# A recurrent stage with its state summed and transposed in two halves, and the shuffle moved

## The chip, the cores and the metric

The kernel runs on one core of a Trainium2 chip. The metric is the device time of one execution in microseconds; before the change it is 3043.02 us, the median of three runs (3042.71 to 3047.3). The engines that matter here are TensorE (PE, matrix products), VectorE (DVE, elementwise work, 32x32 transposes, shuffles between partitions), ScalarE (ACT, sigmoid and tanh), GpSimd (POOL, elementwise work) and SyncE (SP, transfers).

## The reference

The input x has the shape (16, 256, 512), the condition (16, 512). Four blocks are added to x one after the other: an attention over 8 heads, a causal depthwise convolution with 16 taps, a GRU, and an attention over 16 heads. The change touches the GRU alone. It runs over the 256 positions of the second axis, with 16 rows (the batch) and a state h of 512 columns that starts as the condition:

```python
def cell(h, x):
    gi = x @ W_ih + b_ih          # (16, 512) @ (512, 1536)
    gh = h @ W_hh + b_hh
    i_r, i_z, i_n = jnp.split(gi, 3, axis=-1)
    h_r, h_z, h_n = jnp.split(gh, 3, axis=-1)
    r = jax.nn.sigmoid(i_r + h_r)
    z = jax.nn.sigmoid(i_z + h_z)
    n = jnp.tanh(i_n + r * h_n)
    h_new = (1.0 - z) * n + z * h
    return (h_new, h_new)
x = x + _L2_cond_ref(cond_2048, x, L2_cond_W_ih, L2_cond_W_hh, ...)
```

All of it is computed in float32.

## The kernel before

The kernel has four parts in a row: a short set-up, the first attention (`l0_part`), the recurrent stage (`gru_part`), the second attention (`l3_part`). Each part writes out the work of every engine by hand, in order, and binds them with semaphores; there is no planner. A `wait` puts a condition ahead of the next instruction of its engine. The first wait is carried by the instruction itself; further waits are instructions of the engine's sequencer (`EVENT_SEMAPHORE`). Inside hardware loops the values waited for are computed in registers from the loop's variable.

In `gru_part` the 512 columns of a gate are laid out as four groups j of 32 partitions by 128 columns: column 128c + 32j + f of a gate lies at partitions 32j to 32j+31 and free column 32c + f (`group_of`). Each group holds 32 rows: the batch at two time steps (a pair). So each gate is one tile of 128 x 128 in PSUM, filled by four products per k (one for each j), each with a stationary operand of 16 or 32 columns and a moving weight of 128 columns. The even step of a pair (p = 0) uses rows 0 to 15, the odd one (p = 1) rows 16 to 31.

A step t does the following.

- TensorE (`recur`, line 829 on) waits until the turned state `hT` of step t is there (`hT_ready`), and adds h @ W_hh to the gates: 16 products for r, 16 for the hidden part of n, 16 for z, in this order, each over k = 0 to 3 and j = 0 to 3. A product in float32 is two records in the profile, so a gate is 32 records. Then `feed` (line 807 on) adds bias and x @ W_ih for the next pair, six parts a step, from the staged tile `x_st`; its first part of a pair waits for GpSimd's staging.
- ScalarE (line 856 on) takes the sigmoid of r (864), the tanh of a (868) and the sigmoid of z (871).
- VectorE (`step`, line 899 on) computes m = r * (hidden part of n) (907), a = input part of n + m, written to PSUM (911), d = h_swap - n (914), e = d * z (917), h = n + e (919), and turns h in 32x32 blocks into `hT` (922). `hT` has four blocks of columns, one for each k of the next step's products. The transpose waits for `added`, GpSimd's count of read states, and for `h_done`. Then it shuffles h into `h_swap`, with the two halves of 16 rows in each group exchanged (924), so that the next step's rows meet their own state. After that come convolution taps for a later chunk of 32 steps (`conv_tap`, 891): 64 taps are shared over 30 of the 32 steps, so most steps have two, four have three, and the last two of a chunk have none. The last pair of a chunk takes the maxima of the next chunk instead (`greatest`, 897). The last chunk has no taps. VectorE's and GpSimd's loops run over the six middle chunks; the first and last chunks are written out. TensorE's and ScalarE's loops have four steps.
- GpSimd adds the state to x (`add`, 770), once `hT_ready` tells that the transpose of the step is done, and stages the inputs of the next pair (`stage`, 756), once a pair.

Of the kernel before, what the change touches and what calls it, by code (L numbers as in the profile page):

```python
# [25 lines left out]
ALU = mybir.AluOpType  # L26
AX_X = mybir.AxisListType.X

P = 128
B, C, T = 16, 256, 512  # L30
CC, TC = C // P, T // P
# [6 lines left out]
QW = 32  # L38
# [7 lines left out]
def wait(eng, sem, value):  # L46

    if not (isinstance(value, int) and value <= 0):
        eng.wait_ge(sem, value)
# [642 lines left out]
def gru_part(nc, g):  # L692
# [6 lines left out]
    HALF = B  # L699
    SWAP = [(i + HALF) % QW for i in range(QW)]  # L700
    with ExitStack() as ctx:
# [41 lines left out]
        @block.gpsimd  # L743
        def _(pool):
            pool.memset(bias[:, :, :], 0.0).then_inc(setup, 1)
            pool.memset(h_swap[:, :], 0.0).then_inc(setup, 1)
            pool.memset(hT[:, :, :, :], 0.0).then_inc(setup, 1)
            pool.wait_ge(setup, 3)

            pool.tensor_copy(hT[:, 0, :, HALF:QW], g.condT[:, :, :]).then_inc(hT0_ready, 1)  # L750

            def stage(pair, par):


                wait(pool, x_used, pair - 1)
                pool.tensor_copy(x_st[:, par, :, :, :], g.xT[:, :, :, bass.ds(2 * pair, 2)].rearrange("p k b t -> p k t b"))\
                    .then_inc(x_ready, 1)

            def add(t, p):

                q = 1 - p
                if isinstance(t, int):
                    wait(pool, hT_ready, t + 1)
                else:

                    count = pool.snap(pool.to_reg(t + 1))
                    wait(pool, hT_ready, count)
                    t = pool.snap(pool.to_reg(count - 1))
                dst = g.xT[:, :, :, bass.ds(t, 1)].rearrange("p k b o -> p k (b o)")
                pool.tensor_tensor(dst, dst, hT[:, q, :, HALF:QW], ALU.add).then_inc(added, 1)  # L770

            def pair_steps(pair, par, more=True, greatest=0):
                if more:
                    stage(pair + 1, 1 - par)
                wait(pool, max_done, greatest)
                for p in range(2):
                    add(2 * pair + p, p)

            def chunk(n, last=False):
                for q in range(PAIRS):  # L780
                    if q == PAIRS - 1 and not last:
                        pool.wait_ge(conv_done, CONV * (n + 1))
                    pair_steps(PAIRS * n + q, q % 2, not (last and q == PAIRS - 1), TC * (n + 1) if q == 0 else 0)

            pool.wait_ge(copied, 1)
            stage(0, 0)
            chunk(0)
            with pool.Fori(1, CHUNKS - 1) as n:
                chunk(n)
            chunk(CHUNKS - 1, last=True)  # L790
# [11 lines left out]
        @block.tensor  # L802
        def _(pe):
            pe.wait_ge(g.gru_w_loaded, 16 * 2 * TC * GATES)
            pe.wait_ge(bias_loaded, 16 * 2 * GATES)
            pe.wait_ge(hT0_ready, 1)
            pe.wait_ge(ones_ready, 1)

            def feed(pair, par, gate, ks):

                out, done, slots = ((r_ps[par], r_done, slice(0, 1)), (n_ps[par], a_done, slice(1, 3)),
                                    (z_ps[par], z_done, slice(3, 4)))[gate]
                if 0 in ks:
                    if gate == 0:
                        wait(pe, x_ready, pair + 1)

                    wait(pe, done, 2 * (pair - 1))
                    for j in range(TC):
                        pe.matmul(out[QW * j:QW * j + QW, 0:(slots.stop - slots.start) * P], ones[:, :],
                                  bias[:, slots, :].rearrange("p g (c j f) -> p j g c f", c=TC, j=TC)[:, j],  # L820
                                  start=True, stop=True, skip_group_check=True)
                for k in ks:
                    for j in range(TC):
                        last = pe.matmul(out[QW * j:QW * j + QW, 0:P], x_st[:, par, k, :, :],  # L824
                                         group_of(wi[:, k, gate, :], j), start=False, stop=True, skip_group_check=True)
                if gate == 2 and TC - 1 in ks:
                    last.then_inc(x_used, 1)

            def recur(t, p, par):


                wait(pe, hT_ready, t)
                rows = HALF if p == 0 else QW
                state = slice(QW - rows, QW)
                for out, cols, gate, done in ((r_ps[par], slice(0, P), 0, r_in), (n_ps[par], slice(P, 2 * P), 1, n_in),
                                              (z_ps[par], slice(0, P), 2, z_in)):
                    for k in range(TC):
                        for j in range(TC):
                            last = pe.matmul(out[QW * j:QW * j + rows, cols], hT[:, p, k, state],  # L839
                                             group_of(wh[:, k, gate, :], j), start=False, stop=True, skip_group_check=True)  # L840
                    last.then_inc(done, 1)

            def step(pair, par, more):

                for p in range(2):
                    t = 2 * pair + p
                    recur(t, p, par)
                    parts = [(pair + 1, 1 - par, (6 * p + i) // 4, ((6 * p + i) % 4,)) for i in range(6)] if more else []
                    for part in parts:
                        feed(*part)  # L850

            for gate in range(GATES):
                feed(0, 0, gate, range(TC))
            loop(pe, step)

        @block.scalar
        def _(act):
            def step(pair, par, more):
                for p in range(2):
                    t = 2 * pair + p  # L860
                    wait(act, r_in, t + 1)

                    wait(act, m_done, t)
                    act.activation(r_sb[:, :], r_ps[par][:, 0:P], ACT.Sigmoid).then_inc(r_done, 1)  # L864
                    wait(act, a_done, t + 1)

                    wait(act, h_done, t)
                    act.activation(n_sb[:, :], a_ps[:, 0:P], ACT.Tanh).then_inc(n_done, 1)  # L868
                    wait(act, z_in, t + 1)
                    wait(act, e_done, t)  # L870
                    act.activation(z_sb[:, :], z_ps[par][:, 0:P], ACT.Sigmoid).then_inc(z_done, 1)

            loop(act, step)

        @block.vector
        def _(dve):
# [24 lines left out]
            def step(pair, par, taps, after=()):  # L901
                gates = n_ps[par]
                for p in range(2):
                    t = 2 * pair + p
                    wait(dve, n_in, t + 1)
                    wait(dve, r_done, t + 1)
                    dve.tensor_tensor(m_sb[:, :], gates[:, P:2 * P], r_sb[:, :], ALU.mult).then_inc(m_done, 1)  # L907
                    wait(dve, m_done, t + 1)

                    wait(dve, n_done, t)  # L910
                    dve.tensor_tensor(a_ps[:, 0:P], gates[:, 0:P], m_sb[:, :], ALU.add).then_inc(a_done, 1)  # L911
                    wait(dve, n_done, t + 1)
                    wait(dve, swap_done, t)
                    dve.tensor_tensor(d_sb[:, :], h_swap[:, :], n_sb[:, :], ALU.subtract).then_inc(d_done, 1)
                    wait(dve, d_done, t + 1)
                    wait(dve, z_done, t + 1)
                    dve.tensor_tensor(e_sb[:, :], d_sb[:, :], z_sb[:, :], ALU.mult).then_inc(e_done, 1)
                    wait(dve, e_done, t + 1)
                    dve.tensor_tensor(h_sb[:, :], n_sb[:, :], e_sb[:, :], ALU.add).then_inc(h_done, 1)
                    wait(dve, added, t - 1)  # L920
                    wait(dve, h_done, t + 1)
                    dve.transpose(hT[:, 1 - p, :, (1 - p) * HALF:(1 - p) * HALF + QW],  # L922
                                  h_sb[:, :].rearrange("p (c f) -> p c f", f=QW)).then_inc(hT_ready, 1)
                    dve.stream_shuffle(h_swap[:, :], h_sb[:, :], SWAP).then_inc(swap_done, 1)
                    for n, m in taps[p]:
                        conv_tap(n, m)
                    for n, tt in after[p] if after else ():
                        greatest(n, tt)
# [640 lines left out]
```

## Time and profile before

| | us |
|---|---|
| median of three runs | 3043.02 |
| the profiled execution's own time | 3042.79 |
| its span | 3041.0 |
| recurrent stage, from the first product of the state to the last addition | 1142.6 |
| TensorE busy in the stage | 1083.7 |
| VectorE busy in the stage | 849.0 |
| ScalarE busy in the stage | 195.0 |
| GpSimd busy in the stage | 222.7 |

The span is the time between the first and the last instruction of the program in the profiled execution. Busy time is the union of an engine's instructions; with short products that overlap, it doesn't tell that TensorE works at its peak. The 256 steps are alike, so one step in order of time tells most of the stage.

### The profile page before, as it was taken

Reading aid. Unit: us, or ns where it says so; the run is one execution under the profiler, and the core shown is the slowest. Engines: PE = TensorE matmul, PEld = TensorE weight load, DVE = VectorE, ACT = ScalarE, POOL = GpSimd, SP = SyncE. Lnnn points to the kernel's source line nnn. Section 1 sums busy time; section 2 is a strip of 40 time slices with the busy share of each in tenths; the row PEclk is TensorE's granted clock in tenths of the full one; section 3 lists DMA queues with packets and bytes.
Section 4 is the critical chain, followed back from the end, with each engine's and each line's share of the span. In section 5 each row is a group of like instructions: output and inputs, shape, how many; then the busy total and the mean of one; then the engine's idle time right before and its main releaser. Section 6 shows DMA issues by size and latency. Waiting matters only on the chain. (4 is left out here: it accounts for less than half of the span.)

```text
span 3041.0 us, 116061 instructions
## 1 busy us (share of the span) xinstructions
PE 2689.0 (88%) x48668; PEld 1509.0 (50%) x48668; DVE 1971.6 (65%) x3754; ACT 1245.7 (41%) x1939; POOL 635.5 (21%) x736
## 2 busy tenths in 40 slices
PE   6999999999599999999999999938888888888882
PEld 2333333333288888888888888812222222222220
DVE  4555555555677777777777775458766667666660
ACT  1454454444211111111111111105777767777774
POOL 0000000000011222122222221143334343433432
PEclk8999999999799999999999999969999999999997
DMA  1310110110100000000000000023434443444432
GB/s 49 99 51 25 49 48 26 49 46 19 37 5 0 0 1 0 1 0 0 0 1 0 1 0 0 1 62 79 109 103 120 115 110 108 119 110 109 120 82 69
DMA packets 120464, 146.38 MB, mean 48 GB/s; under 512 B 23758, under 2 KB 76912, under 8 KB 120348
## 3 DMA queue, kind: packets, MB, share of 16 engines
q1 hardware_dynamic: 116892, 138.77, 16.5%
q10 hardware_dynamic: 3456, 6.29, 0.7%
q8 instruction: 45, 0.74, 0.1%
q14 instruction: 71, 0.58, 0.1%
HBM read 100.60 MB, written 44.40 MB: 48 GB/s over the span
## 5 line engine op out<-in xcount | busy, mean ns | idle before, releaser
L1357 DVE TENSOR_REDUCE x<-exp_ps 128x2 f32<-128x1024 f32 x352 | 427.1, 1222 | 200.6 <-PE exp_ps L1460 200.6
L839 PE MATMUL exp_ps<-region,gru_hT 128*16 128x128 f32 x16384 | 498.4, 274 | 55.1 <-DVE gru_hT L922 44.8
L839 PEld LDWEIGHTS exp_ps<-region,gru_hT 128*16 128x16 f32 x16384 | 428.3, 103 | 122.7 <-DVE gru_hT L922 122.7
L1303 ACT ACTIVATE region<-exp_ps,x 128x1024 f32<-128x1024 f32 x336 | 370.3, 1109 | 89.5 <-PE exp_ps L1435 89.5
L539 DVE TENSOR_REDUCE l_maxes<-exp_ps 128x2 f32<-128x1024 f32 x176 | 215.3, 1224 | 223.4 <-PE exp_ps L605 221.0
L864 ACT ACTIVATE gru_r<-exp_ps 128x128 f32<-128x128 f32 x256 | 71.2, 278 | 623.2 <-PE exp_ps L839 623.2
L770 POOL TENSOR_TENSOR xT<-xT,gru_hT 128x64 f32 (+1 forms) x256 | 133.6, 522 | 912.1 <-DVE gru_hT L922 896.0
L891 DVE SCALAR_TENSOR_TENSOR xT<-x,condT,xT (+1 forms) x420 | 318.4, 801 | 0.0
L1448 PE MATMUL bank<-region,x 128*17 128x512 f32 x2048 | 282.0, 624 | 8.7 <-ACT region L1303 5.3
L824 PE MATMUL exp_ps<-region,gru_x_st 128*32 128x128 f32 x8192 | 285.8, 273 | 0.0
L839 PE MATMUL bank<-region,gru_hT 128*16 128x128 f32 (+1 forms) x8192 | 270.5, 273 | 0.0
L447 ACT ACTIVATE l_probs<-exp_ps 128x1024 f32<-128x1024 f32 x160 | 163.9, 1024 | 205.1 <-PE exp_ps L611 205.1
L839 PEld LDWEIGHTS bank<-region,gru_hT 128*16 128x16 f32 (+1 forms) x8192 | 227.2, 104 | 0.0
L824 PEld LDWEIGHTS exp_ps<-region,gru_x_st 128*32 128x32 f32 x8192 | 225.9, 110 | 0.1
L1303 ACT ACTIVATE region<-bank,x 128x1024 f32<-128x1024 f32 x176 | 195.7, 1112 | 68.2 <-PE bank L1435 67.4
L1357 DVE TENSOR_REDUCE x<-bank 128x2 f32<-128x1024 f32 x160 | 194.7, 1217 | 38.1 <-PE bank L1460 36.8
L605 PE MATMUL exp_ps<-l_kq 32*128 32x512 f32 x704 | 204.7, 666 | 6.0 <-DVE l_maxes L539 5.3
L868 ACT ACTIVATE gru_n<-bank 128x128 f32<-128x128 f32 x256 | 71.1, 278 | 334.3 <-DVE bank L911 334.3
L1460 PE MATMUL exp_ps<-region 52*128 52x512 f16 x704 | 142.6, 403 | 64.2 <-DMA region<-mask_bias_rows 30.9
L907 DVE TENSOR_TENSOR gru_m<-exp_ps,gru_r 128x128 f32<-128x128 f32 x256 | 74.3, 290 | 153.6 <-PE exp_ps L839 144.6
L611 PE MATMUL exp_ps<-l_kq 32*128 32x512 f32 x640 | 173.3, 618 | 0.0
L1477 PE MATMUL bank<-x 128*128 128x512 f32 x256 | 148.3, 665 | 13.7 <-ACT l_neg_max L1260 10.3
(166 smaller groups left out, 3886.7 us busy)
## 6 DMA issues: line engine op xcount, KB each, us to landing
region<-key_query_scratch SPq DMA_DIRECT2D x128, 192.0 KB
l_rden<-rden_scratch SPq DMA_DIRECT2D x64, 256.0 KB
key_query_scratch<-x SPq DMA_DIRECT2D x48, 256.0 KB, 2.9
key_query_scratch<-region SPq DMA_DIRECT2D x48, 256.0 KB, 2.5
l_out<-x_scratch SPq DMA_DIRECT2D x64, 192.0 KB
l_xin<-in_x SPq DMA_DIRECT2D x16, 512.0 KB, 4.2
l_rden<-rden_scratch SPq DMA_DIRECT2D x128, 64.0 KB, 2.0
l_xres<-in_x SPq DMA_DIRECT2D x16, 512.0 KB, 3.7
```

The lines of the kernel that those rows point to most:

```text
L447: act.activation(probs[:, 2 * (seg % 2) + hp, :, :], tasks.bank_of("st", slot)[:, :, :], ACT.Exp, scale=scale)\
L539: dve.tensor_reduce(maxes[:, half, qt, 2 * hp:2 * hp + 2], tasks.bank_of("max", slot)[:, :, :], AX_X, ALU.max)\
L605: last = pe.matmul(tasks.bank(at["max"])[:, i, :], kq[rows, 1 - par, half, qt * P:qt * P + P], kq[rows, 1 - par, half, :], start=True, sto ...
L611: last = pe.matmul(tasks.bank(at["st"])[:, i, :], kq[rows, par, grp, kt * P:kt * P + P], kq[rows, par, grp, :], start=False, stop=True)
L824: last = pe.matmul(out[QW * j:QW * j + QW, 0:P], x_st[:, par, k, :, :], group_of(wi[:, k, gate, :], j), start=False, stop=True, skip_group ...
L839: last = pe.matmul(out[QW * j:QW * j + rows, cols], hT[:, p, k, state], group_of(wh[:, k, gate, :], j), start=False, stop=True, skip_group ...
L891: dve.scalar_tensor_tensor(out=acc, in0=src, scalar=g.condT[:, tt, tap:tap + 1], in1=more, op0=ALU.mult, op1=ALU.add).then_inc(conv_done, 1)
L1303: act.activation(probs[:, 2 * (seg % 2) + hp, :, :], pairs[ring.place[2 * slot]][:, :, :], ACT.Exp, scale=factors[:, 2:3])\
L1357: dve.tensor_reduce(maxes[:, half, qt, head % HH:head % HH + 2], pairs[ring.place[2 * slot + 1]][:, :, :], AX_X, ALU.max).then_inc(taken[" ...
L1448: last = pe.matmul(o_ps[QW * j:QW * j + VW, :], v_sb[:, par, kt, GH * grp + j, :], probs[:, 2 * (seg % 2) + j // 2, j % 2, :], start=(kt = ...
L1460: last = pe.matmul(pairs[ring.place[2 * slot + 1]][:, hf, :], stack[rows, 1 - par, 1, h, qt * P:qt * P + P], stack[rows, 1 - par, 0, h, :] ...
L1477: last = pe.matmul(out, w_sb[:, "qk".index(kind), part, idx * P:idx * P + P], xn[:, par, part, :], start=(part == 0), stop=(part == CC - 1))
```

## The change

The state is summed in two halves of 64 free columns (k blocks 0 and 1, then 2 and 3), and each half is transposed by an instruction of its own, right behind its sum. `h_done` and `hT_ready` are therefore counted twice a step, and the waits on them (TensorE, ScalarE, GpSimd) count 2t. TensorE waits for the first half, takes the products of r and n over k = 0, 1, waits for the second half, takes those over k = 2, 3, and then z over all k. The wait for `added` stands ahead of the first transpose alone. The shuffle of the previous step's state moves from behind the transpose to behind a, ahead of the wait for tanh; at step 0 it is left out, since the first `h_swap` is loaded. GpSimd's wait value and its register for t are computed another way.

```diff
@@ -760,12 +760,11 @@
 
                 q = 1 - p
                 if isinstance(t, int):
-                    wait(pool, hT_ready, t + 1)
+                    wait(pool, hT_ready, 2 * t + 2)
                 else:
 
-                    count = pool.snap(pool.to_reg(t + 1))
-                    wait(pool, hT_ready, count)
-                    t = pool.snap(pool.to_reg(count - 1))
+                    wait(pool, hT_ready, pool.snap(pool.to_reg(2 * t + 2)))
+                    t = pool.snap(pool.to_reg(t + 0))
                 dst = g.xT[:, :, :, bass.ds(t, 1)].rearrange("p k b o -> p k (b o)")
                 pool.tensor_tensor(dst, dst, hT[:, q, :, HALF:QW], ALU.add).then_inc(added, 1)
 
@@ -828,17 +827,24 @@
 
             def recur(t, p, par):
 
-
-                wait(pe, hT_ready, t)
                 rows = HALF if p == 0 else QW
                 state = slice(QW - rows, QW)
-                for out, cols, gate, done in ((r_ps[par], slice(0, P), 0, r_in), (n_ps[par], slice(P, 2 * P), 1, n_in),
-                                              (z_ps[par], slice(0, P), 2, z_in)):
-                    for k in range(TC):
+                gates = ((r_ps[par], slice(0, P), 0, r_in), (n_ps[par], slice(P, 2 * P), 1, n_in), (z_ps[par], slice(0, P), 2, z_in))
+
+                def products(which, ks):
+                    out, cols, gate, done = which
+                    for k in ks:
                         for j in range(TC):
                             last = pe.matmul(out[QW * j:QW * j + rows, cols], hT[:, p, k, state],
                                              group_of(wh[:, k, gate, :], j), start=False, stop=True, skip_group_check=True)
-                    last.then_inc(done, 1)
+                    if TC - 1 in ks:
+                        last.then_inc(done, 1)
+
+                for half in range(2):
+                    wait(pe, hT_ready, 2 * t + half - 1)
+                    for which in gates[0:2]:
+                        products(which, range(2 * half, 2 * half + 2))
+                products(gates[2], range(TC))
 
             def step(pair, par, more):
 
@@ -864,7 +870,7 @@
                     act.activation(r_sb[:, :], r_ps[par][:, 0:P], ACT.Sigmoid).then_inc(r_done, 1)
                     wait(act, a_done, t + 1)
 
-                    wait(act, h_done, t)
+                    wait(act, h_done, 2 * t)
                     act.activation(n_sb[:, :], a_ps[:, 0:P], ACT.Tanh).then_inc(n_done, 1)
                     wait(act, z_in, t + 1)
                     wait(act, e_done, t)
@@ -909,6 +915,9 @@
 
                     wait(dve, n_done, t)
                     dve.tensor_tensor(a_ps[:, 0:P], gates[:, 0:P], m_sb[:, :], ALU.add).then_inc(a_done, 1)
+                    if not (isinstance(t, int) and t == 0):
+
+                        dve.stream_shuffle(h_swap[:, :], h_sb[:, :], SWAP).then_inc(swap_done, 1)
                     wait(dve, n_done, t + 1)
                     wait(dve, swap_done, t)
                     dve.tensor_tensor(d_sb[:, :], h_swap[:, :], n_sb[:, :], ALU.subtract).then_inc(d_done, 1)
@@ -916,12 +925,15 @@
                     wait(dve, z_done, t + 1)
                     dve.tensor_tensor(e_sb[:, :], d_sb[:, :], z_sb[:, :], ALU.mult).then_inc(e_done, 1)
                     wait(dve, e_done, t + 1)
-                    dve.tensor_tensor(h_sb[:, :], n_sb[:, :], e_sb[:, :], ALU.add).then_inc(h_done, 1)
-                    wait(dve, added, t - 1)
-                    wait(dve, h_done, t + 1)
-                    dve.transpose(hT[:, 1 - p, :, (1 - p) * HALF:(1 - p) * HALF + QW],
-                                  h_sb[:, :].rearrange("p (c f) -> p c f", f=QW)).then_inc(hT_ready, 1)
-                    dve.stream_shuffle(h_swap[:, :], h_sb[:, :], SWAP).then_inc(swap_done, 1)
+                    for half in range(2):
+                        cols = slice(2 * QW * half, 2 * QW * half + 2 * QW)
+                        dve.tensor_tensor(h_sb[:, cols], n_sb[:, cols], e_sb[:, cols], ALU.add).then_inc(h_done, 1)
+                        if half == 0:
+
+                            wait(dve, added, t - 1)
+                        wait(dve, h_done, 2 * t + half + 1)
+                        dve.transpose(hT[:, 1 - p, 2 * half:2 * half + 2, (1 - p) * HALF:(1 - p) * HALF + QW],
+                                      h_sb[:, cols].rearrange("p (c f) -> p c f", f=QW)).then_inc(hT_ready, 1)
                     for n, m in taps[p]:
                         conv_tap(n, m)
                     for n, tt in after[p] if after else ():
```

## Rows read from the trace of the kernel before

**Rows 1.** The page's first line.

```profile
span 3041.0 us, 116061 instructions
```
**Rows 2.** Stretches; columns: busy us (xcount) of PE, PEld, DVE, ACT, POOL, PEclk, DMA.

```profile
838.60:1981.20 1142.60, 1083.68 (x38303) 1013.60 (x38292) 849.00 (x2528) 194.95 (x768) 222.74 (x382) 1.00 0.00 1
```
**Rows 3.** The line of m (L907): durations ns min/median/max; what ended idle time (us, times).

```profile
L907 DVE TENSOR_TENSOR gru_m<-exp_ps,gru_r x256: 276/292/293, 840.7 to 1978.7; 128x128 f32<-128x128 f32 x128
...
  PE exp_ps L839: 144.6, 221
  issue: 9.0, 5
```
**Rows 4.** Timeline, an odd step, two taps; start us, us, engine, line, count, [idle before <-releaser].

```profile
1308.36 0.31 DVE L922 STREAM_TRANSPOSE gru_hT<-gru_h 128x128 f32<-128x128 f32 x1
...
1308.60 0.29 DVE L924 STREAM_SHUFFLE gru_h_swap<-gru_h 128x128 f32<-128x128 f32 x1
...
1308.72 1.95 PE L839 MATMUL exp_ps<-region,gru_hT 128*32 128x128 f32 x64 [0.42 <-DVE gru_hT L922]
1308.80 1.51 DVE L891 SCALAR_TENSOR_TENSOR xT<-x,condT,xT  x2
...
1309.87 0.28 ACT L864 ACTIVATE gru_r<-exp_ps 128x128 f32<-128x128 f32 x1 [2.43 <-PE exp_ps L839]
...
1310.49 1.06 PE L839 MATMUL bank<-region,gru_hT 128*32 128x128 f32 x32
1310.75 0.29 DVE L907 TENSOR_TENSOR gru_m<-exp_ps,gru_r 128x128 f32<-128x128 f32 x1 [0.43 <-PE exp_ps L839]
1311.07 0.30 DVE L911 TENSOR_TENSOR bank<-exp_ps,gru_m 128x128 f32<-128x128 f32 x1
...
1311.40 0.28 ACT L868 ACTIVATE gru_n<-bank 128x128 f32<-128x128 f32 x1 [1.25 <-DVE bank L911]
1311.62 0.28 ACT L871 ACTIVATE gru_z<-bank 128x128 f32<-128x128 f32 x1
...
1311.71 0.29 DVE L914 TENSOR_TENSOR gru_d<-gru_h_swap,gru_n 128x128 f32<-128x128 f32 x1 [0.34 <-ACT gru_n L868]
...
1312.04 0.29 DVE L917 TENSOR_TENSOR gru_e<-gru_d,gru_z 128x128 f32<-128x128 f32 x1
1312.37 0.29 DVE L919 TENSOR_TENSOR gru_h<-gru_n,gru_e 128x128 f32<-128x128 f32 x1
1312.76 0.31 DVE L922 STREAM_TRANSPOSE gru_hT<-gru_h 128x128 f32<-128x128 f32 x1
```
**Rows 5.** Timeline, the even step before it, three taps.

```profile
1304.02 1.94 PE L839 MATMUL exp_ps<-region,gru_hT 128*16 128x128 f32 x64 [0.21 <-DVE gru_hT L922]
1304.10 2.33 DVE L891 SCALAR_TENSOR_TENSOR xT<-x,condT,xT  x3
...
1305.01 0.87 POOL L756 COPY gru_x_st<-xT 128x128 f32 x1
...
1305.67 0.88 PEld L839 LDWEIGHTS bank<-region,gru_hT 128*16 128x16 f32 x32
...
1306.36 0.28 DVE L907 TENSOR_TENSOR gru_m<-exp_ps,gru_r 128x128 f32<-128x128 f32 x1
1306.54 0.12 PEld L819 LDWEIGHTS exp_ps<-gru_bias,gru_ones 128*32 128x32 bf16 x4
...
1307.69 0.62 PE L824 MATMUL exp_ps<-region,gru_x_st 128*32 128x128 f32 x16
```
**Rows 6.** VectorE's groups by shape; columns: busy us, mean ns, idle before.

```profile
L922 DVE STREAM_TRANSPOSE gru_hT<-gru_h 128x128 f32<-128x128 f32 x256 | 79.6, 311 | 29.2 <-DVE gru_h L919 3.3
...
L919 DVE TENSOR_TENSOR gru_h<-gru_n,gru_e 128x128 f32<-128x128 f32 x256 | 74.7, 292 | 8.7
...
L550 DVE TENSOR_TENSOR l_kq<-l_qu,l_mask_bc 128x512 f32<-128x512 f32 x32 | 22.1, 692 | 54.0 <-ACT l_qu L410 54.0
...
L504 DVE TENSOR_TENSOR l_max_rest<-l_max_rest,l_max_spread 128x16 f32<-128x16 f32 x32 | 5.9, 185 | 1.3 <-DVE l_max_spread L502 0.2
```
## The prediction

> **What bounds the kernel now.** I read the page first, then the stage alone, then one step of it. The page gives the span of the profiled execution, 3041.0 us [rows 1]; the execution's own time was 3042.79 us, and the median of the runs shown is 3043.02 us. So the sum below is made against 3042.79, and 0.2 us carries it to the median. The view of busy time over the stage that the diff touches [rows 2] shows 1142.6 us: 38% of the span. TensorE is busy in 1083.7 us of it at a granted clock of 1.00 (2.4 GHz throughout), so it looks like the bound. It isn't quite: busy there means records in flight, and before each step's first product it waits for the transpose of VectorE 0.42 and 0.21 us [rows 4, 5].
>
> The stage is 256 steps that depend on each other. The view of the line of the product m [rows 3] shows who VectorE waited for at that point: in 221 steps for TensorE's products, 5 times for "issue" (the 5 back jumps of its loop, which takes the six middle chunks of 32 steps). The rest are steps in which it was late itself: 28 with three convolution taps instead of two (64 taps over 30 steps makes four such in each of 7 chunks) and a few at the start.
>
> A step with two taps reads, in us after the first product S at 1308.72 [rows 4]: sigmoid of r 1.15, m 2.03, a 2.35, tanh 2.68, sigmoid of z 2.90, d 2.99, e 3.32, h 3.65, transpose 4.04, and the next S 4.40 to 4.41. From transpose to transpose it is 1312.76 - 1308.36 = 4.40. That chain is closed: S, products of r and n, m, a, tanh, d, e, h, transpose, S. It sets the end; what isn't on it costs nothing until it reaches it. Every step of the stage stands once in the total, and the stages before and after share no code with it.
>
> **Part 1: h and the transpose in halves.** Price of a half: a tensor-tensor of 128 columns takes 292 ns, one of 16 columns 185, one of 512 692 [rows 6]. The slopes are 0.96 ns a column (16 to 128) and 1.04 (128 to 512), so 64 columns take 292 - 64 x 1.0 = 0.227 us. The transpose has only one shape here, 311 ns. Its bounds are 0.155 (all of it scales) and 0.311 (nothing does); I take the same 0.066 off, 0.245 us, because its 311 ns lies 19 ns from the 292 of the tensor-tensor, whose slope rows show. For h the same bounds are 0.146 and 0.292.
> On the path stand now h (0.292), the gap to the transpose and the transpose (0.311), and 0.06 us to S (0.37 from the transpose's start). Afterwards: h of the first half 0.227, the same gap (it still carries two waits, `added` and `h_done`: 0.39 from h to transpose against 0.33 from e to h), transpose 0.245, 0.06. Gain: 0.065 + 0.066 = 0.13 us a step.
> The second half follows: an instruction that waits for none starts about 0.06 us before the one before it ends (shuffle at 1308.60, transpose's end 1308.67), so h's second half starts 0.18 us after the first transpose starts, T0; its transpose 0.227 + 0.03 later, at T0 + 0.44; it ends at T0 + 0.69. The new S is T0 + 0.31, so the second half's state is there at S + 0.44 with the release.
>
> **Part 2: TensorE, half by half.** 64 records (32 products of two) run from S to the first of z: 1310.49 - 1308.72 = 1.77 us, 27.7 ns a record [rows 4]. The first half of r and n is 32 records, 0.88 us. The second half is there at S + 0.44: no wait. n ends where it ended, and so m's 2.03 stands. r ends 16 records later, 0.44 us: its sigmoid starts at 1.59 and ends at 1.87. m now has r as its second wait; 0.03 us of release (tanh's end to d) and 0.06 for a second wait (the 0.39 against 0.33 above) make 1.96, 0.07 before 2.03. Hidden, with that margin; each 0.01 us beyond it would cost 2.2 us. z keeps its place, 0.1 us ahead of e. The second wait and its register arithmetic fall into TensorE's stream: today the bias products also carry waits, and their weight load starts at 1306.54, where the load of z ends (1305.67 + 0.88) [rows 5]. So such a wait, once satisfied, costs nothing to 0.01 us. TensorE's own work ends with 1307.69 + 0.62 - 0.22 of tail = 1308.09 [rows 5], 4.07 after the S at 1304.02; the new step of 4.27 still holds it.
>
> **Part 3: the shuffle in the gap of tanh.** a starts at 1311.07, d at 1311.71 [rows 4]: 0.64 us. The shuffle has no wait. Behind the transpose it started 0.24 after that one's start, and the convolution 0.20 after the shuffle's. Behind a I take 0.20; it takes 0.29, and d, which waits for it with its second wait, could go 0.10 later: a + 0.60. Hidden by tanh with 0.04 us to spare. Bounds: start with a's dispatch (0.1, nothing lost), or after a has ended (0.30): d at a + 0.70, 0.06 us lost a step. I take nothing.
>
> **Part 4: what comes later on VectorE and GpSimd.** The convolution was released 0.08 us after S. Now it follows the second transpose by about 0.20: T0 + 0.64 = S + 0.33. It is 0.25 us later against S. In two-tap steps it ended at S + 1.59 (1308.80 + 1.51), now at 1.84, before 2.03. In a three-tap step m came at 1306.36 - 1304.02 = 2.34 [rows 5] and comes at 2.59: such a step gains 0.13 and loses 0.25, +0.12. The five jump steps are the same case, since the two maxima ahead of the jump start later. 28 + 5 = 33 steps.
> GpSimd's addition of the state waits for both halves, 0.44 us more after S than today, and so does the staging copy behind it, which now ends at S + 1.86 (1305.01 + 0.87 [rows 5]) and then at S + 2.3. TensorE needs it at S + 2.52 (the bias load at 1306.54 [rows 5]). Hidden, 0.2 us to spare. Its registers are handled as before.
> The Trainium skill speaks against such splitting: VectorE: DVE Perf Modes, "The TRN2 errata", says that each instruction pays its fixed latency anew, and advises tiles of 512 elements or more. Its formula (N + 151)/0.96 gives 157 ns of fixed term; the trace's 292 ns for 128 columns agrees. Two more instructions would by it be 0.31 us of VectorE a step, which in the 33 late steps makes +0.18 instead of +0.12: 3020 us. In the other steps that time lies in VectorE's wait for m.
>
> **The sum.** 221 x -0.13 = -28.7; 33 x +0.12 = +4.0; the second half of the last state +0.3. Net -24.4: 3042.79 - 24.4 = 3018.4, at the median 3018.6. I say 3018.5. Own range 3011 to 3026 (each 0.03 us a step is 6.6 us).
>
> **Rivals.**
> A, the shuffle is late: it starts only when a has ended, and d moves to a + 0.70. For it: a writes PSUM, and no row shows an instruction without a wait behind such a one. Against: shuffle and convolution both start before their forerunner ends [rows 4]. Price 0.06 x 255 = 15.3: 3033.8. (The Trainium skill, VectorE: DVE Perf Modes, "The DRAIN you can't avoid", has the next operation start only when the pipe is empty. The trace differs behind the transpose: 1308.60 against 1308.67.)
> B, the transpose doesn't shrink: gain 0.066 x 221 = 14.6. The first S is later by 0.066, the second transpose and the convolution by about 0.13: against S the convolution is 0.31 late, the 33 steps lose 0.245 each, 8.1. 3042.8 - 6.2 = 3036.6. That is also the case in which the change hardly does what it says.
> C, the transpose scales wholly (0.155): 0.22 x 221 = 48.6 less some 2: about 2996. Against it: every other row has a large fixed part.
> D, the other side, a wait in mid-stream empties TensorE. If the second half's products start only after the pipe has run dry, that costs the tail (64 records in 1.95 us less 63 x 27.7 ns: 0.20) and the 0.06 of a release, 0.26 us, on n's products and so on m. Then 221 x (0.26 - 0.13) + 4.0 = +32.7: 3075.5. It turns to slower when this bubble is over 0.11 us ((28.7 - 4.0) / 221). For it: the state wait at each step's start does show TensorE idle before it. Against it: there it waits for a real event, and the bias products' waits cost nothing.
>
> **Chances.** The forecast 0.60, A 0.14, B 0.07, C 0.05, D 0.08, something else 0.06 (half of it slower). This kernel's time can be told from no change at about 0.2%, 6 us, that is below 3036.9 or above 3049.1. Faster: 0.60 + 0.14 + 0.05 + half of B and of the rest, 0.86; same 0.04; slower 0.10. Range: the forecast's, A's, and a part of the way to C: 3005 to 3035.
>
> **What would show it.** Right: a mean step of about 4.27 us in two-tap steps; half h near 227 ns, half transpose near 245; the first product 0.31 after the first transpose's start; m still 2.03 after S, with TensorE named as its releaser in some 221 steps; sigmoid of r at 1.59; d still 0.64 after a; three-tap steps at m = S + 2.59. Wrong: d at a + 0.70 with VectorE's own shuffle before it (A); a transpose of 300 ns (B); a gap between record 32 and 33 of a step (D); m released by the sigmoid of r, or TensorE without idle time before S, either of which I count as covered.

## The result, and the profile after

The changed kernel takes 3028.56 us (median of five runs, 3024.68 to 3029.28) against 3043.02: ratio 0.9946, 95% interval 0.9932 to 0.9961 (the two medians alone make 0.9952). On another occasion the same pair gave 3023.76 us against 3045.07 and 0.9929 (0.9915 to 0.9943). So it is faster by 0.5 to 0.7%, 14 to 21 us; forecast were 24.5. One of the eleven executions of the kernel before on that occasion was in a slow state, at 14449.08 us; it is left out here, and 3045.07 is the median of the other ten.

The page's first line of the profiled execution (3029.24 us):

```profile
span 3027.4 us, 116763 instructions
```

The stage, from its first product to the last addition; columns as in [rows 2]:

```profile
840.60:1964.20 1123.60, 1081.84 (x38300) 1013.75 (x38292) 911.27 (x3038) 185.34 (x768) 207.56 (x382) 1.00 0.00 1
```

It took 1142.6 us before [rows 2] and 1123.6 now, 19.0 less; the granted clock is 1.00 in both. VectorE is busy 62 us more. What lies before and after the stage is the same code and took 5 us more in this execution than in that of [rows 1]; the section on the forecast comes back to it.

The line of m, which was [rows 3] before:

```profile
L913 DVE TENSOR_TENSOR gru_m<-exp_ps,gru_r x256: 276/292/293, 842.7 to 1961.1; 128x128 f32<-128x128 f32 x128
...
  PE exp_ps L838: 103.5, 221
  issue: 10.1, 5
```

Still 221 steps in which VectorE waits for TensorE's products at m, 5 jumps; the idle time has shrunk from 144.6 to 103.5 us. An odd step with two taps in the middle of the loop, to be held against [rows 4]:

```profile
1302.31 0.24 DVE L935 STREAM_TRANSPOSE gru_hT<-gru_h 128x64 f32<-128x64 f32 x1
1302.48 0.18 DVE L930 TENSOR_TENSOR gru_h<-gru_n,gru_e 128x64 f32<-128x64 f32 x1
...
1302.61 1.95 PE L838 MATMUL exp_ps<-region,gru_hT 128*32 128x128 f32 x64 [0.52 <-DVE gru_hT L935]
1302.70 0.25 DVE L935 STREAM_TRANSPOSE gru_hT<-gru_h 128x64 f32<-128x64 f32 x1
1302.90 1.52 DVE L897 SCALAR_TENSOR_TENSOR xT<-x,condT,xT  x2
...
1304.20 0.28 ACT L870 ACTIVATE gru_r<-exp_ps 128x128 f32<-128x128 f32 x1 [2.66 <-PE exp_ps L838]
...
1304.38 1.06 PE L838 MATMUL bank<-region,gru_hT 128*32 128x128 f32 x32
1304.63 0.29 DVE L913 TENSOR_TENSOR gru_m<-exp_ps,gru_r 128x128 f32<-128x128 f32 x1 [0.20 <-PE exp_ps L838]
1304.96 0.30 DVE L917 TENSOR_TENSOR bank<-exp_ps,gru_m 128x128 f32<-128x128 f32 x1
...
1305.17 0.30 DVE L920 STREAM_SHUFFLE gru_h_swap<-gru_h 128x128 f32<-128x128 f32 x1
...
1305.37 0.28 ACT L874 ACTIVATE gru_n<-bank 128x128 f32<-128x128 f32 x1 [0.90 <-DVE bank L917]
...
1305.68 0.29 DVE L923 TENSOR_TENSOR gru_d<-gru_h_swap,gru_n 128x128 f32<-128x128 f32 x1 [0.21 <-ACT gru_n L874]
...
1306.01 0.29 DVE L926 TENSOR_TENSOR gru_e<-gru_d,gru_z 128x128 f32<-128x128 f32 x1
1306.33 0.22 DVE L930 TENSOR_TENSOR gru_h<-gru_n,gru_e 128x64 f32<-128x64 f32 x1
1306.80 0.24 DVE L935 STREAM_TRANSPOSE gru_hT<-gru_h 128x64 f32<-128x64 f32 x1 [0.24 <-DVE gru_h L930]
```

From S (1302.61): sigmoid of r 1.59, z's products 1.77, m 2.02, a 2.35, shuffle 2.56, tanh 2.76, d 3.07, e 3.40, half h 3.72. Up to there the step is like the others. Its last line isn't: this is one of six steps, one in each turn of VectorE's loop, in which the first transpose starts 0.47 us behind half h; in the other 186 steps of the loop it is 0.26. The step before it, three taps and even, beside [rows 5]; its last line is its first half of h, whose transpose opens the fence above:

```profile
1297.80 1.94 PE L838 MATMUL exp_ps<-region,gru_hT 128*16 128x128 f32 x64
...
1298.10 2.35 DVE L897 SCALAR_TENSOR_TENSOR xT<-x,condT,xT  x3
...
1300.37 0.28 DVE L913 TENSOR_TENSOR gru_m<-exp_ps,gru_r 128x128 f32<-128x128 f32 x1
...
1302.05 0.22 DVE L930 TENSOR_TENSOR gru_h<-gru_n,gru_e 128x64 f32<-128x64 f32 x1
```

And the new shapes beside [rows 6] (the 204 ns of half h are 224 for the half that waits and 183 for the one that doesn't):

```profile
L935 DVE STREAM_TRANSPOSE gru_hT<-gru_h 128x64 f32<-128x64 f32 x512 | 125.7, 245 | 23.4 <-DVE gru_h L930 1.5
L930 DVE TENSOR_TENSOR gru_h<-gru_n,gru_e 128x64 f32<-128x64 f32 x512 | 104.4, 204 | 8.7
```

Two things in these lines aren't as the forecast had them. Tanh starts 0.41 us after a (1304.96 to 1305.37); it was 0.33 [rows 4]. And the transpose starts 0.26 us after half h (1302.05 to 1302.31), where 0.33 was expected. (12 steps of the loop lose 0.22 to 0.25 us at one place each, six of them as the last line of the step above shows; the kernel before had such steps too, 7 of 0.36 and 8 of 0.1. Both make about 3 us in all. Their cause stays open.)

In the written-out first chunk the second of these differs. a, tanh, half h and transpose of a step there:

```profile
958.50 0.30 DVE L917 TENSOR_TENSOR bank<-exp_ps,gru_m 128x128 f32<-128x128 f32 x1
...
958.91 0.28 ACT L874 ACTIVATE gru_n<-bank 128x128 f32<-128x128 f32 x1 [0.90 <-DVE bank L917]
...
959.87 0.23 DVE L930 TENSOR_TENSOR gru_h<-gru_n,gru_e 128x64 f32<-128x64 f32 x1
960.20 0.25 DVE L935 STREAM_TRANSPOSE gru_hT<-gru_h 128x64 f32<-128x64 f32 x1
```

Tanh is 0.41 behind a here as well, but the transpose is 0.33 behind half h. (Only VectorE's code is written out in this chunk; ScalarE's loop runs here too. Over the whole stage tanh is 0.41 to 0.42 behind a in 248 steps, those of ScalarE's loop, and 0.33 in the other 8. The transpose is 0.33 behind half h in 61 of the 63 written-out steps ahead of another one.)

The 255 intervals from first product to first product, by kind, in us (sum, and mean of one):

| | steps | before | after |
|---|---|---|---|
| first four | 4 | 18.9 | 18.8 |
| written-out chunks, without three-tap steps | 55 | 242.9 (4.416) | 239.7 (4.359) |
| loop, without three-tap and jump steps | 163 | 720.0 (4.417) | 699.4 (4.291) |
| three-tap | 28 | 128.6 (4.592) | 131.7 (4.702) |
| jump | 5 | 27.7 (5.531) | 28.8 (5.764) |
| all | 255 | 1138.0 | 1118.5 |

### The profile page after: what moved, and what is told of

Its sections match the earlier page's. It is cut to its first block and busy times, and to the rows that moved or that the text cites. A ratio compares the mean times of both kernels' runs of the same rounds, so it can differ in the third digit from the quotient of the medians.

```text
span 3027.4 us, 116763 instructions
## 1 busy us (share of the span) xinstructions
PE 2699.3 (89%) x48668; PEld 1511.6 (50%) x48668; DVE 2034.2 (67%) x4264; ACT 1235.9 (41%) x1939; POOL 620.0 (20%) x736
## 5 line engine op out<-in xcount | busy, mean ns | idle before, releaser
L769 POOL TENSOR_TENSOR xT<-xT,gru_hT 128x64 f32 (+1 forms) x256 | 118.2, 462 | 910.1 <-DVE gru_hT L935 892.8
L913 DVE TENSOR_TENSOR gru_m<-exp_ps,gru_r 128x128 f32<-128x128 f32 x256 | 74.3, 290 | 113.5 <-PE exp_ps L838 103.5
```

## The experiments

Theory 1, formed from these lines: what differs is which instruction carries a wait, that is, which one is held until the semaphore has the value. In ScalarE's loop the wait on `h_done` needs 2t, and a register operation for it stands between the two waits of tanh. It takes over the wait on `a_done`, so that it runs only after a: the sequencer's own instructions of ScalarE in the window 1305.2 to 1305.45 show one that starts at 1305.3, right behind the end of a (1305.26), and in the same gap of the kernel before there is none.

```profile
L49 ACTq ALU_OP  x1: 38/38/38, 1305.3 to 1305.3; - x1
```

On VectorE the same thing helps: in the loop a register operation carries `added` and the transpose carries `h_done`; in the written-out steps, with constants, `h_done` is a sequencer's instruction of its own, as it is in the kernel before. VectorE's sequencer between h and the first transpose, in a loop step and a written-out step of the changed kernel and in a loop step of the kernel before:

```profile
L49 DVEq FUSED_REGOPS  x1: 53/53/53, 1302.2 to 1302.2; - x1
...
L49 DVEq EVENT_SEMAPHORE  x1: 21/21/21, 960.1 to 960.1; - x1
...
L49 DVEq EVENT_SEMAPHORE  x1: 21/21/21, 1312.7 to 1312.7; - x1
```

Rivals: the shuffle behind a delays a's signal (theory 2), or the numbers lie in the halves themselves. All times below are medians beside runs of the kernel before on the same chip (3045.07, 3044.33 and 3044.54 us: a0, a1, a2 and b1 beside the first, b2, b3, a3 and c1 beside the second, c3 and c4 beside the third); "stage" is from first product to first product of the last step, 1138.0 and 1118.5 us above.

| run | stage us | time us | ratio to before (95%) |
|---|---|---|---|
| a0_changed_again | 1118.2 | 3023.76 | 0.9929 (0.9915 to 0.9943) |
| a1_tanh_value | 1100.1 | 3004.33 | 0.9868 (0.9852 to 0.9884) |
| a2_shuffle_back | 1123.5 | 3027.87 | 0.9948 (0.9932 to 0.9964) |
| b1_tanh_register | 1173.1 | 3079.31 | 1.0118 (1.0100 to 1.0135) |
| b2_wait_order | 1119.8 | 3025.37 | 0.9940 (0.9926 to 0.9953) |
| b3_shuffle_moved | 1133.1 | 3040.57 | 0.9989 (0.9980 to 0.9998) |
| a3_r_whole | 1117.4 | 3027.03 | 0.9945 (0.9931 to 0.9959) |
| c1_all | 1105.5 | 3012.23 | 0.9900 (0.9886 to 0.9913) |
| c3_best | 1094.7 | 3002.20 | 0.9854 (0.9840 to 0.9868) |
| c4_e_halves | 1105.3 | 3011.89 | 0.9893 (0.9875 to 0.9911) |

**a0_changed_again**, the changed kernel unchanged.

> The changed kernel as it is, beside the kernel before on the same chip. In its first profile the stage from the first product of step 0 to that of step 255 took 1118.5 us against 1138.0 before (-19.5), while the whole execution gained only 13.6; TensorE's low-clock periods outside the stage summed to 282 us against 248. Theory A (the give-back is no effect of the change but the clock of that execution): the stage again near 1118.5, and low-clock time outside it that varies from run to run and doesn't follow the kernel. Theory B (the change brings more low clock to the later stage): again some 30 us more low-clock time than the kernel before, and a gain of 13 to 15 us only.

The stage repeats within 0.3 us. The mean granted clock of a whole execution was 0.954 to 0.959 over six of the changed kernel, and 0.952 to 0.959 over ten of the kernel before on the same chip; the latter ranged from 3039.9 to 3050.9 us. Of their spans, all but the stretch from the first product of step 0 to that of step 255 took 1903.0 us in the profiled execution of the kernel before (clock 0.959), 1909.0 in the first one of the changed kernel (0.953) and 1904.9 in this one (0.955). So of the 6.0 us lost there in the first execution only 1.9 are lost in the second, with the same code, as theory A has it. That the clock moves it is read from these few executions; no run changes the clock alone.

**a1_tanh_value.**

```diff
+                    turned = 2 * t if isinstance(t, int) else act.snap(act.to_reg(2 * t))
                     wait(act, r_in, t + 1)
...
-                    wait(act, h_done, 2 * t)
+                    wait(act, h_done, turned)
```

> The changed kernel, but ScalarE computes the value 2t of its wait on h_done at the start of the step instead of between the wait on a_done and that on h_done. Theory 1 (register arithmetic that stands behind a wait takes that wait over, so it runs only after a is done and delays tanh by 0.08 us in each of the 248 steps of ScalarE's loop): tanh 0.33 us after a instead of 0.41, the stage 20 us shorter (1098.5 between first products), the time 3008 to 3010. Theory 2 (the shuffle behind a delays the signal that a is done): tanh stays at a + 0.41 and the time at 3028.6.

VectorE and ScalarE in one step: a, shuffle, tanh, d.

```profile
1302.09 0.30 DVE L918 TENSOR_TENSOR bank<-exp_ps,gru_m 128x128 f32<-128x128 f32 x1
...
1302.30 0.30 DVE L921 STREAM_SHUFFLE gru_h_swap<-gru_h 128x128 f32<-128x128 f32 x1
...
1302.42 0.28 ACT L875 ACTIVATE gru_n<-bank 128x128 f32<-128x128 f32 x1 [0.82 <-DVE bank L918]
...
1302.73 0.29 DVE L924 TENSOR_TENSOR gru_d<-gru_h_swap,gru_n 128x128 f32<-128x128 f32 x1
```

Tanh is 0.33 behind a, with the shuffle in its place. The stage lost 18.1 us (20 expected) and the whole 19.4 against a0_changed_again. (The 3008 to 3010 us expected for the whole started from 3028.6 us; beside this run the changed kernel took 3023.76.) Theory 2 is out, and d is at a + 0.64, as before the change: the shuffle is hidden. In the trace of this run tanh carries the wait on `a_done` again, and the wait on `h_done` has become an instruction of the sequencer that is over before a starts.

**a2_shuffle_back**, the shuffle again behind the second transpose.

> The changed kernel with the shuffle back behind the (second) transpose; halves, order of products and ScalarE's waits as changed. Theory 1 (register arithmetic on ScalarE): tanh still 0.41 after a; the convolution starts 0.2 us later, so the 28 three-tap steps and 5 jump steps lose 0.2 each: stage +6.6 (1125 between first products), time 3035. Theory 2 (the shuffle delays a's signal): tanh at a + 0.33, stage 1105, time 3015.

Tanh stayed at a + 0.41. The three-tap steps went from 4.70 to 4.87 and nothing else moved by more than 1 us: +5.3 us, 6.6 expected. The time was 3027.87 us, 4.1 more than a0_changed_again. The rest of the steps hid the shuffle in VectorE's wait for m.

**b1_tanh_register**, the kernel before with the suspected cost: `h_done` counts by two, ScalarE waits for 2t, and VectorE's own wait value 2t + 2 is computed behind a.

```diff
-                    wait(act, h_done, t)
+                    wait(act, h_done, 2 * t)
...
+                    summed = value(2 * t + 2)
...
-                    dve.tensor_tensor(h_sb[:, :], n_sb[:, :], e_sb[:, :], ALU.add).then_inc(h_done, 1)
+                    dve.tensor_tensor(h_sb[:, :], n_sb[:, :], e_sb[:, :], ALU.add).then_inc(h_done, 2)
...
-                    wait(dve, h_done, t + 1)
+                    wait(dve, h_done, summed)
```

> The kernel before with one thing of the changed one alone: h_done counts by two and ScalarE waits for 2t, so that its loop needs a register operation between the waits of tanh; VectorE's own wait value is computed ahead, in the gap of tanh. No halves, shuffle where it was. Theory 1: tanh at a + 0.41, +0.08 x 248 = +20 us: 3063, 0.6 to 0.7% slower than the kernel before. Theory 2: tanh at a + 0.33 and 3043.

a, tanh, d, e, h of one step:

```profile
1303.33 0.30 DVE L911 TENSOR_TENSOR bank<-exp_ps,gru_m 128x128 f32<-128x128 f32 x1
...
1303.74 0.28 ACT L868 ACTIVATE gru_n<-bank 128x128 f32<-128x128 f32 x1 [1.34 <-DVE bank L911]
...
1304.05 0.29 DVE L916 TENSOR_TENSOR gru_d<-gru_h_swap,gru_n 128x128 f32<-128x128 f32 x1 [0.43 <-ACT gru_n L868]
...
1304.38 0.29 DVE L919 TENSOR_TENSOR gru_e<-gru_d,gru_z 128x128 f32<-128x128 f32 x1
1304.77 0.29 DVE L921 TENSOR_TENSOR gru_h<-gru_n,gru_e 128x128 f32<-128x128 f32 x1
```

Tanh is at a + 0.41, so the register operation does it without halves and without the shuffle behind a. But the stage grew by 35 us, not 20: h starts 0.39 behind e, where it was 0.33 [rows 4]. The h that adds two carries no wait here; its wait on `e_done` became an instruction of the sequencer (21 ns at 1304.7), the same 0.07 us as at the transpose. 0.08 + 0.07 a step is about what the loop shows (4.417 to 4.555, 0.14). So the expectation of 3063 us was missed, at 3079.31, by this second cost.

**b2_wait_order**, the kernel before with the two waits ahead of its transpose exchanged.

```diff
+                    summed, read = value(t + 1), value(t - 1)   # behind a
...
-                    wait(dve, added, t - 1)
-                    wait(dve, h_done, t + 1)
+                    wait(dve, h_done, summed)
+                    wait(dve, added, read)
```

> The kernel before, whole state, shuffle where it was; only the two waits ahead of the transpose change places, so that the instruction itself carries h_done, which comes last, and the sequencer waits for added, which has long come; both values are computed ahead, in the gap of tanh. Theory 1 (a late wait that the sequencer handles alone costs 0.07 us more than one that the instruction carries): h to transpose 0.33 us instead of 0.40, in all 255 steps, -18 us: stage 1120, time 3025. Theory 2 (the 0.40 is the transpose's own, since it needs the whole of h): nothing moves, stage 1138.

h and the transpose:

```profile
1307.96 0.29 DVE L921 TENSOR_TENSOR gru_h<-gru_n,gru_e 128x128 f32<-128x128 f32 x1
1308.28 0.31 DVE L924 STREAM_TRANSPOSE gru_hT<-gru_h 128x128 f32<-128x128 f32 x1
```

0.32 apart instead of 0.39 [rows 4], the stage 18.2 us shorter. In the loop the run also moves the computing of two values; in the written-out steps these are constants and the order alone differs, and there a step went from 4.416 to 4.338 us. This one exchange is worth almost as much as the whole change was in the stage (19.5).

**b3_shuffle_moved**, the kernel before with the shuffle's move alone.

> The kernel before with the shuffle's move alone. Theory 1: it lies within tanh (d still 0.64 us after a), two-tap steps stay 4.39 to 4.41, the convolution starts 0.2 us earlier and the 28 three-tap steps gain 0.15 to 0.2 each, the jumps 0.2: stage -6 (1132), time -0.2%. Rival (the shuffle is late behind the instruction that writes PSUM): d at a + 0.70, stage 1138 - 6 + 15 = 1147.

```profile
1300.78 0.30 DVE L911 TENSOR_TENSOR bank<-exp_ps,gru_m 128x128 f32<-128x128 f32 x1
...
1300.99 0.30 DVE L914 STREAM_SHUFFLE gru_h_swap<-gru_h 128x128 f32<-128x128 f32 x1
...
1301.42 0.29 DVE L917 TENSOR_TENSOR gru_d<-gru_h_swap,gru_n 128x128 f32<-128x128 f32 x1
```

d is at a + 0.64 with the shuffle done behind the instruction that writes PSUM: it starts 0.21 after a. Stage -4.9 us (-6 expected), all of it in the three-tap steps (4.59 to 4.43).

**a3_r_whole**, the changed kernel with all of r before n.

```diff
-                    for which in gates[0:2]:
-                        products(which, range(2 * half, 2 * half + 2))
-                products(gates[2], range(TC))
+                    products(gates[0], range(2 * half, 2 * half + 2))
+                for which in gates[1:3]:
+                    products(which, range(TC))
```

> The changed kernel with all 16 products of r first (the wait for the second half between its k = 1 and k = 2), then n, then z. The prediction had r's lateness (sigmoid at S + 1.57) covered and the second half there at S + 0.4, just before r's third group of products is due at 0.44. Theory 1: sigmoid of r at S + 1.13 again, n and m unmoved at 2.01, stage unchanged at 1118 to 1119. Rival (m's release by n hides a cost of r): the stage moves by more than 2 us either way; if the second half comes late for r's second part, E2 and m shift by that much.

The sigmoid of r went back to S + 1.13, m stayed at 2.01, the stage moved by 0.8 to 1.1 us. Taking r and n half by half neither costs nor brings anything: TensorE works through four products of each k in 0.22 us, and the second half of the state is there before r's third k is due.

**c1_all**, a1_tanh_value, a3_r_whole, and the exchanged waits with their values computed ahead, behind a.

> The best version that the runs so far point to: the changed kernel with ScalarE's value computed ahead (stage 1100.1 alone), the two waits ahead of the first transpose in the order h_done, added with values computed ahead, which should take 0.07 us off each of the 56 steps of the two written-out chunks and nothing in the loop, and r whole first. Stage 1100.1 - 3.9 = 1096; time about 3000.

a, shuffle, tanh, d in a loop step:

```profile
1303.41 0.30 DVE L918 TENSOR_TENSOR bank<-exp_ps,gru_m 128x128 f32<-128x128 f32 x1
...
1303.72 0.30 DVE L923 STREAM_SHUFFLE gru_h_swap<-gru_h 128x128 f32<-128x128 f32 x1
1303.75 0.28 ACT L875 ACTIVATE gru_n<-bank 128x128 f32<-128x128 f32 x1 [1.33 <-DVE bank L918]
...
1304.13 0.29 DVE L926 TENSOR_TENSOR gru_d<-gru_h_swap,gru_n 128x128 f32<-128x128 f32 x1
```

A miss: the stage is 1105.5 us for 1096, the time 3012.23 for 3000. The values that I had VectorE compute stood between a and the shuffle and took its sequencer 0.22 us. In this step the shuffle started at a + 0.31, and now it did hold up d, at a + 0.72, though tanh was in its place again. (In the loop the shuffle is at a + 0.28 in about half the steps and a + 0.31 in the other half, d at a + 0.68 to 0.72.) That is the delay of rival A, brought about by another cause. The written-out steps, with constants, gained as expected (4.359 to 4.212).

**c3_best**, a1_tanh_value, and the exchange only where the values are constants:

```diff
+                            waits = ((h_done, 2 * t + 1), (added, t - 1))
+                            for sem_, count in waits if isinstance(t, int) else waits[::-1]:
+                                wait(dve, sem_, count)
```

> c1_all lost in the loop what it should have kept: the values computed ahead on VectorE stood between a and the shuffle (0.22 us), the shuffle started 0.09 us later and d with it. So here: ScalarE's value computed ahead as in a1_tanh_value; the order h_done, added of the waits ahead of the first transpose only in the written-out steps, where the values are constants; in the loop the order of the changed kernel, whose register operation carries the wait on added. Theory 1: stage 1100.1 - 0.07 x 56 = 1096, time 3000 to 3003. Rival: the written-out steps don't gain in this form and the stage stays at 1100.

1094.7 us, 43.3 less than the kernel before: 3002.20 us, the fastest of all. Written-out steps 4.201, loop steps 4.214. Beside b2_wait_order, in which the transpose carries `h_done` too and nothing is split, this tells what the halves are worth: 0.137 us a written-out step and 0.122 a loop step, for 0.13 forecast, and 25.1 us of the stage (the shuffle's move included).

**c4_e_halves**, c3_best with e in halves as well (ScalarE then waits for 2t on `e_done` too, with the value of `h_done`).

> c3_best with e in two halves as well: e, h, transpose of the first 64 columns, then the same of the second. Theory 1 (VectorE's order is the next bound): S comes 0.066 us earlier after e, but the second transpose 0.24 later, so the convolution ends 0.30 later against S (2.11 instead of 1.81) and m starts at 2.04 instead of 2.01: two-tap steps gain 0.03, 33 three-tap and jump steps lose 0.2: stage 1096 + 1 (between 1094 and 1100), no faster. Rival (only the chain to the first transpose counts, as in the forecast for the change): -0.066 x 250 = -16, stage 1080.

e, h, transpose of the first half, e of the second, the taps:

```profile
1304.93 0.23 DVE L929 TENSOR_TENSOR gru_e<-gru_d,gru_z 128x64 f32<-128x64 f32 x1
1305.19 0.22 DVE L931 TENSOR_TENSOR gru_h<-gru_n,gru_e 128x64 f32<-128x64 f32 x1
1305.52 0.25 DVE L938 STREAM_TRANSPOSE gru_hT<-gru_h 128x64 f32<-128x64 f32 x1
1305.69 0.18 DVE L929 TENSOR_TENSOR gru_e<-gru_d,gru_z 128x64 f32<-128x64 f32 x1
...
1306.37 1.52 DVE L898 SCALAR_TENSOR_TENSOR xT<-x,condT,xT  x2
```

Slower than c3_best by 9.7 us, 10.6 in the stage, where 1 was expected: 1105.3 us lies outside the 1094 to 1100 that the expectation gave. Written-out steps gained (4.201 to 4.160). The three-tap steps lost 0.28 each, 7.8 us in all: VectorE's taps start 0.26 us later against S. And in the loop the transpose fell back to 0.33 behind h (1305.19 to 1305.52), which ate the gain (4.214 to 4.236): in the trace the register operation now runs ahead of h, carries no wait, and `h_done` is the sequencer's again. I had left that out of the expectation.

## Why the forecast was right, and where it wasn't

The direction, the mechanism of the halves and the stated range held (3028.56 in 3005 to 3035); the size was 24.4 us forecast, 19.5 in the stage, 14.5 between the first medians. The range held with the help of its width: 3028.56 is above the 3011 to 3026 that the main case had been given, in the part that stood there for rival A, which did not come true. And that loop steps came out as forecast is luck, as two of the points below say.

- **Halves.** 227 and 245 ns forecast, 224 and 245 measured; the first product 0.30 after the first transpose's start. Right. So rival B (no shrinking) and C (full scaling) are out.
- **The gap from h to the transpose** was to stay. In the loop it fell by 0.07 us, in the written-out chunks it stayed. The forecast had said that the 0.39 came from two waits, but not which of the two the instruction carries, and that is what counts (b2_wait_order).
- **TensorE.** z's products at S + 1.77, m at 2.02, r's sigmoid at 1.59: right, and the 64 records of a step still take 1.95 us, so the second half's wait leaves no gap. Rival D is out.
- **The shuffle in the gap of tanh**: hidden, right (a1_tanh_value, b3_shuffle_moved). Yet d moved to a + 0.72, close to rival A's a + 0.70. A's number came true for another reason: the shuffle had ended at 1305.47, 0.21 us before d, and what was late was tanh. Whoever looked at d alone would have called A shown.
- **The step that failed** is the one that isn't in the list of parts: "the waits count 2t" was priced on TensorE and GpSimd and not on ScalarE, where it puts a register operation behind the wait on a. Price 0.08 us in 248 steps: 20 us by the steps, 18.1 measured (a1_tanh_value). In the loop it ate what the cheaper wait ahead of the transpose gave: 4.27 us a two-tap step was forecast and 4.28 measured (the median; 4.291 is the mean with the odd steps), by luck, with two errors of 0.07 and 0.08 that cancel. In the written-out chunks nothing cancels it: 55 steps gained 0.057 each instead of 0.13, 4 us short.
- **Late steps.** m at S + 2.57 (1300.37 - 1297.80) for 2.59; +0.11 us a three-tap step for +0.12. The lateness against S is right; the price of the whole step holds by the same cancelling, since a1_tanh_value, without the late tanh, has 4.637 against the 4.592 before, +0.045. The jumps lost 0.23 instead of 0.12, 0.5 us.
- **The rest.** 163 x -0.126 - 3.2 + 3.1 + 1.1 - 0.1 = -19.6. What the medians show less or more than this (-14.5, -21.3) lies outside the stage as far as the profiled executions tell (1903.0, 1909.0 and 1904.9 us there), and executions of the kernel before differ by 11 us among themselves. That the clock granted to the two attentions makes it fits the figures at a0_changed_again and is not shown beyond them.

## What to carry over

When an edit changes what a wait compares with, look at how the value comes about: in this kernel arithmetic on a loop's variable was an instruction of the sequencer, it took over the wait that stood before it, and behind a wait that comes last it was on the path. Compute such values where the engine waits anyway, but not ahead of something that has just enough room. Of two waits ahead of one instruction, let the instruction carry the one that comes last; it costs nothing to write, and here it was worth 18 us, where splitting the work, with the shuffle moved, was worth 25 (b2_wait_order, c3_best).

## What the runs showed that I had not expected

- A wait that the sequencer handles as its own instruction costs 0.07 us more than one that the instruction carries (transpose 0.39 and 0.32, h 0.39 and 0.33).
- A register operation behind the last wait costs 0.08 us on ScalarE (tanh 0.41 and 0.33 behind a), and the h that adds two to its semaphore carries no wait (b1_tanh_register).
- A half h with a wait takes 224 ns, the one without a wait 183.
